# Routing comparisons in two halves of the columns, and two weight preparations exchanged between the routing stage and the experts' end

## What is computed

```python
capacity = int(math.ceil(T / E * CAPACITY_FACTOR))      # T = 2048 tokens, E = 8: 320
probs = jax.nn.softmax(tokens @ router_w.T, axis=-1)
top1_idx, top1_prob = jnp.argmax(probs, axis=-1), jnp.max(probs, axis=-1)
order = jnp.lexsort((-top1_prob, top1_idx))
sorted_e = top1_idx[order]
pos_in_group = jnp.arange(T) - start[sorted_e]
keep = jnp.zeros((T,), bool).at[order].set(pos_in_group < capacity)
final_e = jnp.where(keep, top1_idx, 0)
for e in range(E):
    h = relu(tokens @ W1[e] + b1[e]); y = h @ W2[e] + b2[e]
    out = out + jnp.where((final_e == e)[:, None], y, 0.0)
```

## Time and profile before

| what | value |
|---|---|
| time, median of 3 runs | 1243.11 us (1241.47 to 1243.6) |
| the profiled execution, its own time | 1242.15 us |
| its span | 1240.4 us |
| busy over the span | PE 1064.9 (86%), DVE 959.5 (77%), ACT 693.5 (56%), POOL 383.5 (31%) |
| routing block, from its first TensorE product to SyncE's first DMA of the experts' block | 575.06 to 634.11 us |
| experts' block, to VectorE's first instruction of the recurrence | 634.11 to 788.07 us |

### The profile page before, as it was taken

How to read it: one execution, slowest core, us unless ns; L and a number is a source line. 1 busy time by engine, 2 the same in 40 slices (tenths; PEclk the granted TensorE clock), 3 DMA queues, 4 the chain that set the end, 5 groups by cost and what they waited for, 6 DMA issues and landing times. The chain is left out here.

```text
span 1240.4 us, 30089 instructions
## 1 busy us (share of the span) xinstructions
PE 1064.9 (86%) x10763; PEld 855.5 (69%) x10763; DVE 959.5 (77%) x2126; ACT 693.5 (56%) x1461; POOL 383.5 (31%) x535
## 2 busy tenths in 40 slices
PE   5899989989998799986279999489999859998696
PEld 3578878778787577765267777377788637776585
DVE  7588878877887588997838884569998648898597
ACT  3354544444545255555637776368778626555584
POOL 5123222221230256552220000423421225655232
PEclk9899999999999899997569999699999969999899
DMA  7000000200000230004336531300000000000011
GB/s 263 10 10 2 10 13 2 84 3 2 3 2 2 87 121 12 22 9 174 136 110 246 178 110 49 112 18 19 29 14 21 1 14 24 12 22 10 18 56 47
DMA packets 33493, 64.29 MB, mean 52 GB/s; under 512 B 7524, under 2 KB 23268, under 8 KB 30308
## 3 DMA queue, kind: packets, MB, share of 16 engines
q1 hardware_dynamic: 31844, 58.57, 13.5%
q0 software_dynamic: 1536, 4.20, 1.0%
HBM read 43.03 MB, written 12.39 MB: 45 GB/s over the span
## 5 line engine op out<-in xcount | busy, mean ns | idle before, releaser
L1151 ACT ACTIVATE ca_pth<-ca_turned 77x512 f16<-77x512 f32 x128 | 75.9, 593 | 99.8 <-PE ca_turned L1293 99.8
L395 ACT ACTIVATE wa_probs<-wa_scores,wa_minus_top 128x192 f32<-128x192 f32 x256 | 83.3, 437 | 80.5 <-DVE wa_minus_top L488 80.5
L1094 POOL TENSOR_TENSOR ca_z<-ca_z,ca_top 128x308 f32<-128x308 f32 x128 | 88.2, 701 | 112.4 <-DVE ca_top L1189 112.4
L351 POOL TENSOR_TENSOR wa_q<-wa_by_cos,wa_by_sin 128x256 f32<-128x256 f32 x32 | 23.4, 732 | 265.4 <-DVE wa_by_sin L483 265.4
L1194 DVE SCALAR_TENSOR_TENSOR ca_ptl<-ca_turned,ca_pth 77x512 f16<-77x512 f32 x128 | 87.0, 680 | 20.0 <-ACT ca_pth L1151 20.0
L1293 PE MATMUL ca_turned<-ident,ca_probs 128*77 128x128 f32 x512 | 87.0, 294 | 14.0 <-ACT ca_probs L1143 13.9
L406 ACT ACTIVATE wa_pth<-wa_turned 128x384 f16<-128x384 f32 x128 | 58.4, 506 | 72.2 <-PE wa_turned L715 72.2
L1293 PEld LDWEIGHTS ca_turned<-ident,ca_probs 128*77 128x77 f32 x512 | 57.7, 152 | 44.6 <-ACT ca_probs L1143 24.6
L640 PE MATMUL wa_scores<-wa_xh,wa_wh 128*128 128x256 f16 x256 | 71.1, 278 | 10.4 <-DVE wa_wl L467 8.8
L488 DVE TENSOR_REDUCE wa_minus_top<-wa_scores 128x2 f32<-128x384 f32 x128 | 62.3, 548 | 20.6 <-PE wa_scores L703 18.5
L715 PE MATMUL wa_turned<-ident,wa_probs 128*128 128x128 f32 x512 | 68.3, 275 | 7.8 <-ACT wa_probs L395 3.9
(11 more groups left out here) (388 smaller groups left out, 3643.8 us busy)
## 6 DMA issues: line engine op xcount, KB each, us to landing
ex_stage<-in_ew SPq DMA_DIRECT2D x16, 1024.0 KB, 7.0
slots<-slots_zeros SPq DMA_DIRECT2D x10, 512.0 KB, 6.2
ca_xs<-tokens SPq DMA_DIRECT2D x16, 256.0 KB, 2.4
ex_xe<-slots SPq DMA_DIRECT2D x11, 320.0 KB, 3.3
slots<-ex_y SPq DMA_DIRECT2D x9, 320.0 KB
wa_x_stage<-in_xt SPq DMA_DIRECT2D x8, 256.0 KB, 3.1
tokens<-in_x SPq DMA_DIRECT2D x1, 2048.0 KB, 15.3
ca_w<-in_xw SPq DMA_DIRECT2D x2, 1024.0 KB, 6.9
```

The lines of the kernel that those rows point to most:

```text
L395: ins = act.activation(probs[2 * (u % 2) + t][:, h, t * WINDOW:t * WINDOW + SPAN], s_bank[i][:, t * SPAN:(t + 1) * SPAN], ACT.Exp, bias=mi ...
L1094: pool.tensor_tensor(z[k][:, heads], z[k][:, heads], top[:, k, heads].unsqueeze(2).broadcast_to((P, UH, CTX)), ALU.subtract).then_inc(shif ...
L1151: act.activation(pth[k][0:CTX], t_bank[k][0:CTX], ACT.Copy, scale=PSCALE).then_inc(probs_high, 1)
```

## The change

Four edits.

1. **Halves.** The comparisons run over two halves of the columns (tiles 0 to 7, then 8 to 15; h = 0, 1): all 16 rows for the first half, then all 16 for the second. The products of a half go into a PSUM bank of its own, so ranks and slots of the first half are picked and given during the second half's comparisons (`sort_out(0)`, `give_slots(0)`), and GpSimd scatters tiles 0 to 7 as soon as it has them, tiles 8 to 15 after the second half's slots. VectorE begins with the first two pieces of `keys`. `ahead` gets 6 buffers of half the size.
2. **Exchange.** `gates.rates`, `power_of_base` and the whole of `binary` (split, add_sizes, scale_sizes) leave the end of the routing block and go to the end of the experts' block. The split of W_g goes from there to the routing block.
3. W_g (2 MB) is loaded with the other early loads, ahead of w_in.
4. In the recurrence GpSimd does `root_in(0)` ahead of `gates.gather(.., 1)`.

```diff
+ROUTED = TILES // 2
+ROWS_AHEAD = 6
...
-        ahead = [sb(f"ahead{k}", [P, TOKENS], BF16) for k in range(3)]
+        ahead = [sb(f"ahead{k}", [P, ROUTED * P], BF16) for k in range(ROWS_AHEAD)]
...
-            pool.wait_ge(slots_ready, 1)
             for j in range(TILES):
+                if j % ROUTED == 0:
+                    pool.wait_ge(slots_ready, j // ROUTED + 1)
                 pool.indirect_dma_start(...)
...
+            keep_keys(0)
             act.wait_ge(consts, 13)
+            act.wait_ge(keys_ready, 2)
+            act.wait_ge(minus_ready, 1)
+            sign_row(0, 0)
+            keep_keys(1)
+            for n in range(1, len(SIGNED_TILES)):
+                sign_row(n, 0)
             act.wait_ge(keys_ready, 4)
...
+            for n in range(len(SIGNED_TILES)):
+                sign_row(n, 1)
             ahead_of_experts["scalar"](act)
-            binary.split(act)
...
+            for h in range(2):
+                dve.wait_ge(keys_ready, 2 * h + 2)
+                test(0, h)
+                test(1, h)
+                if h:
+                    sort_out(0)
+                own_rows_gap(h)
+                for n in range(2, len(TESTED_TILES)):
+                    test(n, h)
+                    if n == 2 and h:
+                        give_slots(0)
+                        then(dve.tensor_scalar(first_end[:], upto[:, ROUTED - 1:ROUTED], float(BASE), None, ALU.add))
+                    if n == 3:
+                        own_rows(h, own_before, before, ALU.is_ge)
+                    if n == 5:
+                        own_rows(h, own_after, after, ALU.is_gt)
+            sort_out(1)
+            give_slots(1)
...
             ahead_of_experts["vector"](dve)
-            binary.scale_sizes(dve, k_bank)
...
+            for h in range(2):
...
+                for j in range(TILES):
...
+                    if j == 1 and h:
+                        count(0)
+                own_blocks(h)
+            count(1)
-            binary.add_sizes(pe, k_bank)
...
@@ the first experts' preparations, inside the routing block
-            gates.rates(dve)
+            gates.split_low(dve)
...
-            gates.power_of_base(act)
+            gates.split_high(act)
...
@@ the end of the experts' block
-            gates.load_gates(sp, w_g)
...
-            gates.split_high(act, w_g)
+            gates.power_of_base(act)
+            binary.split(act)
...
             take_y(end - 1)
-            gates.split_low(dve, w_g)
+            gates.rates(dve)
+            binary.scale_sizes(dve, u_bank)
...
             turn_y(end - 1)
+            binary.add_sizes(pe, u_bank)
...
         sp.dma_start(self.hid[:], hid_dram).then_inc(self.hid_loaded, 16)
+        sp.dma_start(self.w_g[:], w_g_dram).then_inc(self.g_loaded, 16)
         sp.dma_start(self.w_in[:], w_in_dram).then_inc(self.w_loaded, 16)
...
+            root_in(0)
             gates.gather(pool, slots, slot, 1)
-            root_in(0)
             root_in(1)
```

More of the change, by code:

```diff
@@ L1503, in route @@
     with ExitStack() as ctx:
-        binary.hold(ctx, nc)
         def sb(name, shape, dt=F32):
@@ L1722, in _, with test @@
-            then(dve.tensor_tensor(place[:], place[:], base[:], ALU.mult))
-            dve.tensor_tensor(slot[:], place[:], place_side[:], ALU.add).then_inc(slots_ready, 1)
-            then(dve.tensor_scalar(over[:], steps[:], upto[:, TILES - 1:TILES], None, ALU.is_lt))
+            def test(n, h):
+                j, q = TESTED_TILES[n], h * len(TESTED_TILES) + n
+                row = ahead[q % ROWS_AHEAD]
+                lo, left, right = sides(j, h)
+                if q >= ROWS_AHEAD:
+                    dve.wait_ge(row_done, rows_with(TESTED_TILES, q - ROWS_AHEAD))
+                for side_of, test_of in ((left, ALU.is_gt), (right, ALU.is_ge)):
+                    if side_of.start < side_of.stop:
+                        ins = dve.tensor_scalar(row[:, side_of.start - lo:side_of.stop - lo], keys[:, side_of], key[:, j:j + 1], None, test_of)
+                ins.then_inc(tested, 1)
@@ new lines, in sort_out @@
+            def sort_out(h):
+                t = tiles(h)
+                dve.wait_ge(ranks, h + 1)
+                then(dve.tensor_tensor(own[:, t], r_bank[h][:, 0:ROUTED], onehot[:, t], ALU.mult))
+                then(dve.tensor_reduce(rank[:, t], own[:, t], AX.X, ALU.add))
+                then(dve.scalar_tensor_tensor(out=side[:, t], in0=rank[:, t], scalar=float(CAP), in1=others[:, t],
+                                              op0=ALU.is_lt, op1=ALU.mult))
+                then(dve.tensor_scalar(base[:, t], side[:, t], -1.0, 1.0, ALU.mult, ALU.add))
+                dve.tensor_copy(base_bf[:, t], base[:, t]).then_inc(base_ready, 1)
+                then(dve.tensor_tensor(place_side[:, t], start_slot[:, t], rank[:, t], ALU.add))
+                then(dve.tensor_tensor(place_side[:, t], place_side[:, t], side[:, t], ALU.mult))
@@ L1725, in _ @@
+            sort_out(1)
+            give_slots(1)
+            then(dve.tensor_tensor(last_end[:], upto[:, ROUTED - 1:ROUTED], upto[:, TILES - 1:TILES], ALU.add))
+            then(dve.tensor_scalar(over[:], steps[:], last_end[:], None, ALU.is_lt))
             then(dve.tensor_reduce(many[:], over[:], AX.X, ALU.add))
@@ L1779, in sem @@
             return ctx.enter_context(nc.semaphore("ex_" + name))
+        binary.hold(ctx, nc)
+        gates.hold(ctx, nc)
         starts = sb("starts", [P, 1], I32)
```

185 lines of the change are left out of this document (90 added, 95 removed).

## The result

The changed kernel took 1245.44 us, median of 20 runs (1243.89 to 1246.94), beside 1242.65 us (1240.72 to 1243.65) for the kernel before in 20 runs: a ratio of 1.0023, 95% interval 1.0017 to 1.0030. It is slower by 2.8 us. The profiled execution has a span of 1242.6 us, against 1240.4.

What follows compares the result with a forecast made beforehand. It took the binary weights' chain to end the routing block, the scatter close behind, and GpSimd's gathers the experts' block. Terms -7.1, +8.6 and 0 sum to +1.5 us: median 1244.6 us, range 1240.6 to 1248.6.

Steps and rivals of the forecast that it cites:

- Term 1: Routing block: the last slots come 3.5 us later, for added VectorE instructions, a new wait and contention with scatters.
- Term 2: Start of the experts: the first expert product comes 7.1 us earlier, at 631.0 against 638.07, as scatters end earlier.
- for landing and block end I take 2.0 us: Routing block's end: time from the last scatter's end to SyncE's mark, 2.0 us, bounded to 1.2 and 2.9.
- the second chain ends the block, and the first is close behind it: Routing block's end, kernel before: binary weights' chain, done at 633.73, ends the block; the scatter's chain is close behind.
- I priced it where it meets `ex_xe`, at +0.6 us: Start of the experts: the 320 expert rows queue behind the rest of the weights' reload, +0.6 us.
- Term 3: Experts' end: the binary weights' chain, 17.72 us long, moves there and delays VectorE's next block by 8.6 us.
- the clock rival: Experts' end: TensorE at 2.4 GHz shrinks the sums, delay there only +2.4 us, total 1238.4 us; chance 12%.
- Term 4: Recurrence: the first root ahead of the second gather wins and loses nothing, 0 us.
- the mark that I set was 13: Routing block: the first eight scatters taking over 13 us would decide that they starve beside VectorE's tests.
- The slow halves: Routing block: ScalarE's half rows cost more than 2.3 us each and set the end, 1248 us; chance 8%.
- 14, 13 and 8: Shares for slower by over 0.2%: 14 from the forecast, 13 from starving scatters, 8 from slow halves; given as 36%.
- the starving rival: Routing block: scatters get through only between VectorE's rows of tests; net +3.6 to +5.9 us, 1246.7 to 1249.0; chance 15%.

Runs made afterwards that it cites:

- `binary_to_end_only`: The kernel before with only the binary weights' chain and the rates moved to the experts' end, comparisons at full width; ratio 1.0084 to the kernel before.
- `reload_late`: The changed kernel with the reload of expert weights issued behind the first load of expert rows; median 1245.61 us.
- `binary_split_early`: The changed kernel with only ScalarE's sign split of the binary matrix back in the routing block; median 1238.32 us.
- `no_scatters_ahead`: The changed kernel with GpSimd waiting for both halves' slots before the first scatter; 9.7 us above the changed kernel.
- both kernels with two or three moves: The changed kernel with early sign split and late reload, 1239.49 us; the same with W_g's low half at the experts' start too, 1238.73 us.
- `changed_again`: The changed kernel without any edit, run once more among the experiments; 1248.96 us, ratio 1.0050 to the kernel before.
- `pause_after_four`: The changed kernel with the second gather ahead of the first root, GpSimd pausing after four scatters for the second ranks; five spans 1242.4 to 1243.8 us, three 1247.4 to 1248.7.

## Why the prediction came out as it did

I forecast 1244.6 us and the median was 1245.44, the net change +1.5 against a measured +2.8. The mechanism was as forecast; two sizes were off, and they partly cancelled. The traces put the change's own part at +3.4 us, and that the profiled execution was only 2.2 us longer is owed to the 1.15 us ahead of the routing block. So part of the closeness is luck.

- *Term 1, the last slots, +3.5*: measured +3.3. First test at 581.25 and first slots at 598.79 are, with 1.15 us added for the earlier start, 582.4 and 599.9, forecast as 582.4 and 600.4; the wait ahead of `sort_out(0)` was 1.08 us, forecast as over 1 us.
- *Term 2, the first expert product, -7.1*: measured -4.17. The scatters were right: last end at 624.2 in the same count, 624.4 forecast. The step that failed is "for landing and block end I take 2.0 us", bounded by 1.2 and 2.9. It was 5.87. I had bounded it from the window without traffic at 632 to 634 and from the chain's end at 633.73, and concluded that "the second chain ends the block, and the first is close behind it". The kernel before itself had 3.26 us from scatter to mark, and this, I held, was the chain's. `binary_to_end_only`, with no chain there, has 3.24; `reload_late`, `binary_split_early`, `no_scatters_ahead` and both kernels with two or three moves have 3.24 or 3.25. That is the price of a landing and a block's end without a collision: 1.3 us more than I took. The window without traffic told when the data had moved, not when the block had ended: in the changed kernel 1.8 us still pass from the last landing to the mark. The other 2.6 us are the reload. I priced it where it meets `ex_xe`, at +0.6 us; it met the last two scatters first, which the block must wait for, and since all was over by the mark, `ex_xe` had no queue (3.80 us from mark to product, 3.96 before).
- *Term 3, the experts' end, +8.6*: measured +7.73. The chain took 16.81 us, not 17.72, and nearly all of the difference is in the 256-column products: 5.26 us instead of 6.16. This is the clock rival in a small dose. These windows of the changed kernel:

```profile
776.00:784.00 8.00, 6.06 (x29) 6.09 (x29) 3.24 (x19) 5.50 (x3) 2.14 (x3) 0.50 0.13 39
784.00:788.00 4.00, 4.00 (x13) 3.37 (x13) 0.17 (x1) 0.00 (x0) 0.00 (x0) 0.51 0.00 0
788.00:792.00 4.00, 2.02 (x10) 1.44 (x8) 1.47 (x7) 0.00 (x0) 0.10 (x1) 1.00 0.00 0
```

  The granted clock stood at 1.2 GHz while the one-column products ran and rose to 2.4 GHz at about 788, within the second part. Of the nine traces with the whole chain at the experts' end three have 5.1 to 5.4 us for that part and six, `changed_again` among them, 6.4 to 6.7 us, with 18.3 to 18.6 us from `re_low` to the next block. So the forecast's size fits the six, and the 0.9 us are not sure.
- *Term 4, the recurrence, 0*: the stretch from its first instruction to the next load is 0.56 us shorter in the first trace, and the gather's place doesn't order it (222.66 in `changed_again`, 222.81 and 222.83 in the two kernels with the gather ahead, 221.57 in `pause_after_four`, which has it ahead too). Zero holds within 1 us.
- *The rivals*: in the changed kernel's profile the scatters did not starve beside the tests. The first eight took 11.4 us (599.95 to 611.32), the mark that I set was 13. In four other kernels with the same code there they took 13.4 to 14.7 us, over that mark: one scatter was held until the row of tests was over, and in `binary_split_early` only two of the eight were out by then, as the rival has it. So whether GpSimd gets in between two tests that follow at once, which the prediction left open, is answered both ways, and the rival is real for part of the executions. The slow halves were not there: ScalarE's half rows cost 2.2 us each and its last ended at 604.7, ahead of VectorE. Two slips in the prediction's arithmetic change nothing: 14, 13 and 8 are 35%, not 36, and with none of the eight out the starving rival's own working gives 635.7 us for the first product, -2.4 and not -2.7.

What I had no case for is the late read of the ranks. With it the changed kernel's first product comes 64.25 us behind the first load, later than before. It stood in five of the eleven profiled executions whose comparisons run in halves and whose scatters begin between the halves, and at the same place each time. Its cause stays open: the way GpSimd's scatters and VectorE's tests fall on each other, TensorE's event (its products paused as well) and something of the chip that no row names are all still possible. The first is favoured by the rows, and the kernel with a pause doesn't decide.

The change's own part is therefore, by the traces: +7.7 us for a chain put where 9.4 us hide it instead of the 18 from `re_low` to the mark, -4.2 us for scatters begun between the halves; the small rest is in stages that the change leaves alone or nearly so. The experiment that leaves ScalarE's part of that chain where it was takes 7.2 us off the experts' end, and its time is below both kernels' (ratio to before 0.9968, interval 0.9956 to 0.9980).

## What to carry to other kernels

When a block seems to end with one chain, subtract the other one's last issue from the block's end and see whether that gap recurs elsewhere: a landing, which has no row of its own among the engines' instructions, hides in it, and two tied chains must both be moved. Whatever moves a DMA earlier moves it against other traffic: look up which large load goes out within its landing time. When a chain over several engines moves to a place with little cover, leave behind the links that need nothing from the new place; here ScalarE's split was one, and moving it back was worth 7 us.

## What the hardware showed beyond that

- A late consumer: VectorE's read of a finished result came 5.0 us behind TensorE's last product in five executions, 0.9 us in four and 0.03 to 0.06 us in the others; the changed kernel itself shows both ends (39.49 and 34.29 us behind the first load).
- The time ahead of the change differs between kernels whose code there is the same, and goes with the granted clock over the first 100 us: first load at 573.5 to 573.9 us with 0.98 (five traces), 574.4 with 0.97 (two), 575.0 to 575.5 with 0.95 (three, the kernel before among them), 575.5 to 576.7 with 0.93 (four). The two kernels that were profiled twice repeated their clock; why it differs stays open. Differences of 1 to 3 us between whole times need the first load's time beside them.
- An indirect scatter of GpSimd took 0.96 us at rest, and beside VectorE's tests and splits anything from 0.96 to 4.33 us (`binary_split_early`, the second), by how the two rows of instructions fell on each other: it went through between tests that follow at once, or waited for the last of nine. The sixteen ended between 49.2 and 54.4 us behind the first load in kernels that differ around them by little, part of it for the late read.
